# First cross attention of a decoder kernel: transposing a unit's attention weights as row halves of the array, with the copies on two engines

## The reference

```
scores  = einsum('bqhd,bkhd->bhqk', Q, K) / SCALE
weights = jax.nn.softmax(scores, axis=-1)
attn    = einsum('bhqk,bkhd->bqhd', weights, V).reshape(b, lq, h * d)
out     = attn @ Wo.T + bo
```

## Time and profile before

| | |
|---|---|
| median of 3 runs | 2547.52 us (2543.78 to 2550.26) |
| the profiled execution | 2545.91 us, with a span of 2543.8 us |
| busy share of the span | PE 89%, PEld 74%, DVE 64%, ACT 45%, POOL 29% |
| the 64 units of `stage_b` | scores from 810.6 us, last transposes at 1102.9 us |

### The profile page before, as it was taken

One profiled execution on the slowest core, in us unless ns is written; L12 is line 12 of the kernel. 1 busy time (PEld: TensorE's weight loads), 2 busy tenths in 40 slices (PEclk: granted clock), 3 DMA queues, 4 the chain that ended last, 5 costly groups with the idle time before them and its releaser, 6 DMA issues. The chain is left out here.

```text
span 2543.8 us, 62618 instructions
## 1 busy us (share of the span) xinstructions
PE 2262.9 (89%) x26115; PEld 1870.4 (74%) x26115; DVE 1633.5 (64%) x3577; ACT 1135.2 (45%) x3176; POOL 736.0 (29%) x866
## 2 busy tenths in 40 slices
PE   5798989998898999955998589989997899999998
PEld 4677877777785888844887366666775788888887
DVE  6766666667644667656784455655665777777776
ACT  4444443443324555522554356656674233333332
POOL 2333333424323433331565433420111011110110
PEclk9899999999999999966999799999998899999999
DMA  5000000100103000020442300000000000000001
GB/s 159 4 17 30 32 31 11 35 27 25 51 3 111 10 18 18 14 80 26 119 119 34 105 2 2 2 2 2 2 2 14 19 26 26 26 20 26 26 7 34
DMA packets 87961, 83.36 MB, mean 33 GB/s; under 512 B 27264, under 2 KB 83456, under 8 KB 86272
## 3 DMA queue, kind: packets, MB, share of 16 engines
q1 hardware_dynamic: 81536, 70.98, 8.9%
q0 software_dynamic: 6144, 8.39, 1.9%
HBM read 68.71 MB, written 10.65 MB: 31 GB/s over the span
## 5 line engine op out<-in xcount | busy, mean ns | idle before, releaser
L2653 PE MATMUL bank<-f_XH,f_wp 128*128 128x512 f32 x1088 | 364.6, 396 | 5.9 <-DVE f_XL L2763 5.9
L797 DVE SCALAR_TENSOR_TENSOR a_acc<-a_praw,a_convw,a_acc 128x256 f32<-128x256 f32 x345 | 206.7, 600 | 97.6 <-ACT a_acc L957 89.4
L2653 PEld LDWEIGHTS bank<-f_XH,f_wp 128*128 128x128 f32 x1088 | 208.4, 192 | 48.6 <-issue 5.0
L2653 PEld LDWEIGHTS bank<-f_wp,f_Hp 128*128 128x128 f32 x1632 | 214.3, 191 | 27.5 <-DVE X L2790 16.0
L2653 PE MATMUL bank<-f_wp,f_Hp 128*128 128x256 f32 x1632 | 218.5, 283 | 16.2 <-DVE X L2790 15.4
L2653 PE MATMUL bank<-f_XL,f_wp 128*128 128x512 f32 x544 | 215.9, 397 | 0.0
L2837 POOL TENSOR_TENSOR f_wp<-wa,f_wp 128x768 fp32r<-128x768 f32 x34 | 62.9, 1849 | 521.6 <-ACT f_wp L2803 521.6
L2788 DVE SCALAR_TENSOR_TENSOR X<-bank,f_w,X 128x256 f32<-128x256 f32 x512 | 211.4, 475 | 0.0
L2826 ACT ACTIVATE f_Hp<-f_H 128x512 fp32r<-128x512 f32 x136 | 85.9, 632 | 223.8 <-DVE f_H L2775 223.8
L2824 ACT ACTIVATE f_G<-bank 128x512 f32<-128x512 f32 x136 | 81.3, 598 | 165.2 <-PE bank L2653 165.2
L2777 DVE TENSOR_TENSOR f_Hp<-f_H,f_Hp 128x512 fp32r<-128x512 f32 x136 | 94.1, 692 | 94.9 <-ACT f_Hp L2826 94.9
(11 more groups left out here) (389 smaller groups left out, 5530.2 us busy)
## 6 DMA issues: line engine op xcount, KB each, us to landing
wa<-in_c_w SPq DMA_DIRECT2D x64, 256.0 KB, 3.4
wa<-in_f_gu SPq DMA_DIRECT2D x34, 256.0 KB, 2.8
wb<-grown SPq DMA_DIRECT2D x4, 1536.0 KB, 6.9
a_KQg<-grown SPq DMA_DIRECT2D x4, 1536.0 KB, 6.4
wa<-in_f_d SPq DMA_DIRECT2D x34, 128.0 KB, 2.8
a_E<-decays SPq DMA_DIRECT2D x16, 256.0 KB, 4.0
X<-in_x SPq DMA_DIRECT2D x4, 512.0 KB, 5.2
wa<-in_a_wqkv SPq DMA_DIRECT2D x1, 2048.0 KB, 8.8
```

The costliest lines, as they stand in the source:

```text
L797: i = v.e.scalar_tensor_tensor(A_, praw[:, c, :, j:j + BT_], convw[:, c, j:j + 1], A_, ALU.mult, ALU.add)
L2653: i = t.e.matmul(out_, lhsT[x], rhs[y], start=n == 0 and k == 0, stop=n == 2 and k == nk - 1, skip_group_check=True)
```

## The change

The transposes of a unit become one step `("turn", u)` with two banks, which stand for the two halves of the 128 tokens and no longer for the two `par`. Each of the 8 blocks of 128x77 is transposed as two blocks of 64x77, the first 64 tokens in the upper half of the array's rows, the other 64 in the lower half, each against a 64x64 part of the identity. The step waits for both banks before its first transpose, and both banks are filled by its last two. `b_PT` becomes two buffers of the same total size. DVE copies the first half's bank and ACT, right after its exps of the unit behind, copies the second half's bank.

```
-            PT = [t_(f"PT{i}", [HALF, 2, 2, P]) for i in range(NPB)]
+            PT = [t_(f"PT{i}", [HALF, 2, 2, 2, P]) for i in range(NPB // 2)]
-                order += [("turn", u - 2, par) for par in range(2)] * (0 <= u - 2 < U) + [("scale", u - 1)] * (0 <= u - 1 < U)
+                order += [("turn", u - 2)] * (0 <= u - 2 < U) + [("scale", u - 1)] * (0 <= u - 1 < U)
+                elif what == "turn":
+                    for half in range(2):
+                        at[s + (half,)] = banks[4 + turns % 4]
+                        at[s + (half,)].turn(*k, half)
+                        turns += 1
+                    continue
-            square = lambda ap: ap[0:HALF, :].rearrange("p (a b c) -> p a b c", a=2, b=2)
+            halves = [slice(0, P // 2), slice(P // 2, P)]
+            by_head = lambda ap: ap[0:HALF, :].rearrange("p (r a b c) -> p r a b c", r=2, a=2, b=2)
 # tensor, turn
-                        free(t, *s)
-                        for j in range(2):
-                            for hf in range(2):
-                                i = t.e.transpose(square(b.ap)[:, j, hf, :], Pm[u % NPB][:, par, j, hf * HALF:(hf + 1) * HALF], ident)
-                        i.then_inc(b.filled, 1)
+                        for half in range(2):
+                            free(t, *s, half)
+                        for par in range(2):
+                            for j in range(2):
+                                for hf in range(2):
+                                    for half, rows_ in enumerate(halves):
+                                        b = at[s + (half,)]
+                                        i = t.e.transpose(by_head(b.ap)[:, par, j, hf, :],
+                                                          Pm[u % NPB][rows_, par, j, hf * HALF:(hf + 1) * HALF],
+                                                          ident[rows_, rows_], tile_position=(rows_.start, 0))
+                                        if (par, j, hf) == (1, 1, 1):
+                                            i.then_inc(b.filled, 1)
 # tensor, mix: reads PT[u % 2][:, par, j, hf, :]
 # vector, turn
-                        filled(v, *s)
-                        v.e.tensor_copy(PT[2 * (u % 2) + par][:], square(b.ap)).then_inc(b.emptied, 1)
+                        filled(v, *s, 0)
+                        v.e.tensor_copy(PT[u % 2][:, :, :, :, halves[0]], by_head(b.ap)).then_inc(b.emptied, 1)
 # scalar, exp of unit u waits for both halves of turn u - 4; and new:
+                    elif what == "turn":
+                        u, b = s[1], at[s + (1,)]
+                        if u > 1:
+                            filled(c, "mix", u - 2)
+                        filled(c, *s, 1)
+                        c.e.activation(PT[u % 2][:, :, :, :, halves[1]], by_head(b.ap), ACT.Copy).then_inc(b.emptied, 1)
```

More of the change, by code:

```diff
@@ L1329, in tensor @@
                     elif what == "turn":
-                        _, u, par = s
+                        u = s[1]
                         t.wait_ge(scaled.sem, scaled.at[u,])
-                        free(t, *s)
-                        for j in range(2):
-                            for hf in range(2):
-                                i = t.e.transpose(square(b.ap)[:, j, hf, :], Pm[u % NPB][:, par, j, hf * HALF:(hf + 1) * HALF], ident)
-                        i.then_inc(b.filled, 1)
+                        for half in range(2):
[10 more added lines that the diff above has]
+                                            i.then_inc(b.filled, 1)
                     elif what == "mix":
@@ L1348, in tensor @@
                                     i = t.e.matmul(b.ap[rows(par), j * P:(j + 1) * P], V[:, n // TB, hf, 4 * q + 2 * j + par, :],
-                                                   PT[2 * (u % 2) + par][:, j, hf, :], start=hf == 0, stop=hf == 1,
+                                                   PT[u % 2][:, par, j, hf, :], start=hf == 0, stop=hf == 1,
                                                    tile_position=(0, par * XD), skip_group_check=True)
@@ L1403, in vector @@
                     elif what == "turn":
-                        _, u, par = s
+                        u, b = s[1], at[s + (0,)]
                         if u > 1:
                             filled(v, "mix", u - 2)
-                        filled(v, *s)
-                        v.e.tensor_copy(PT[2 * (u % 2) + par][:], square(b.ap)).then_inc(b.emptied, 1)
+                        filled(v, *s, 0)
+                        v.e.tensor_copy(PT[u % 2][:, :, :, :, halves[0]], by_head(b.ap)).then_inc(b.emptied, 1)
                     elif what == "mix":
@@ L1454, in scalar @@
                         if u >= NPB:
-                            filled(c, "turn", u - NPB, 1)
+                            for half in range(2):
+                                filled(c, "turn", u - NPB, half)
                             c.wait_ge(inverted.sem, inverted.at[u - NPB,])
```

## The result

The changed kernel took 2522.73 us in the median of 4 runs (2520.89 to 2528.92), the kernel before 2548.76 us beside it. The ratio is 0.991, with a 95% interval of 0.989 to 0.992: 20 to 27 us faster. The forecast was 2518 us, 29 us less, with a range of 2511 to 2535 us.

The account below looks back on a forecast made before the run. PE was taken as the bound. 54 units at 0.446 us (24.1 us) and 5.0 us for the last ten turns gave 29.1 us off 2545.91; with 1.6 us for the median, the forecast was 2518 us, range 2511 to 2535.

Parts of the forecast that it names:

- The start of the transposes: On PE, transposes start 0.63 us behind the score instead of 0.73, since both now share a tile shape.
- the mix: On PE, the mix starts 1.27 us into the round instead of 1.75, 0.48 us less.
- Rival A: On PE, the gap between score and transposes stays, as transposes may count as another shape: 2527 us, 15%.
- The price of a pair: On PE, two half-row transposes run beside each other and a pair goes by in 0.069 us.
- the upper bound: A pair of transposes at 0.112 us: mix at 1.57 us, 0.18 us a unit, 2536 us in all.
- PE stays the bound: In plain rounds of 3.21 us, POOL's scale feeds the transposes in time, by 0.12 us.
- rival B: PE no longer the bound: a longer copy, reciprocal and scale loop costs 0.1 to 0.2 us a round, 2524 to 2531 us, 12%.
- The three rounds with a layernorm: Of every eight rounds, three with waits on POOL gain 0.33 + 0.48 + 0.36 = 1.17 of 12.54 us.
- The last ten units: Ten turns at the stage's end, where queries are missing, together gain 5.0 us.
- rival C: PE's clock falls to half earlier, in the three rounds of 3.48 us, as PE waits more: 2526 us, 7%.
- Rival D: On PE, the two transposes of a pair do not overlap: 14 us slower, 2561 us, 6%.
- E: No change: PE held by the number of instructions, 0.062 us a transpose, 0.03 us gained a unit: 2545 us, 2%.

Follow-up runs that it names:

- experiment 5: Changed kernel with PE doing the mix before the transposes in units 8 to 51: 2524.47 us in one run.
- experiment 9: Changed kernel with 64 instead of 77 stationary columns in each transpose, part of the attention left out: 2509.93 us in one run.
- experiment 4: Changed kernel with 8 of a unit's 16 transposes taking 128 stationary columns instead of 77: 2517.74 us in one run.
- experiment 8: Changed kernel with DVE's reciprocal ahead of the copy and the next stage's layernorm moved a round later: 2511.05 us, ratio 0.986 to the kernel before.
- experiment 1: Changed kernel with half-row transposes but both copies on DVE, none on ACT: 2543.94 us, ratio 0.999 to the kernel before.
- experiments 6: Changed kernel with DVE's reciprocal of the unit behind moved ahead of the copy of the transposes: 2520.12 us, ratio 0.988 to the kernel before.
- 7: Changed kernel with the first score matmuls of units 57 to 63 repeated to fill PE's waits: 2521.93 us, ratio 0.989 to the kernel before.
- experiment 3: Changed kernel with all 8 transposes of one row half first, then the other 8, instead of alternating: 2541.82 us in one run.
- experiment 2: Kernel before, whole-array transposes kept, only the second bank's copy moved to ACT: 2539.76 us, ratio 0.998 to the kernel before.

## Why the prediction was right, and where not

**The start of the transposes** at 0.63 us and **the mix** at 1.27 were worked out, 0.63 and 1.26 to 1.27 measured; the round 3.20 against 3.21. Rival A is out, and experiment 5 shows the rule at work: one more change of shape in a round costs the 0.15 us.

**The price of a pair**, 0.069 us, was right. That it hangs on the number of stationary columns is shown by experiment 9 for 64 against 77 (0.056 us, near the lower bound of 0.0575). The rule behind it, a pair goes by the wider of load and pass with the load priced by its columns, does not hold to the end: the upper bound, 0.112, was taken from matmuls, and experiment 4 shows that a half-row transpose with 128 columns goes by in about 0.067 us.

**PE stays the bound** by 0.12 us was worked out, with 0.05 us from POOL's end to the transposes taken off. In plain rounds the scale ends 0.15 to 0.17 us before the transposes start, so the margin is 0.10 to 0.12, and rival B is out. The prediction did not price what the second engine is worth: with both copies on DVE the margin is negative, and of 21.6 us in units 8 to 55 only 9.1 are left. The copy on ACT is not a detail of the change but more than half of it.

**The three rounds with a layernorm**, 1.17 us gained, one wait kept and one gone: 12.54 - 11.37 = 1.17 us measured. Experiment 8 shows that POOL's order sets the kept wait.

**The last ten units**, 5.0 us, is the term that was mis-sized: 1.0 us measured. The loop of these rounds shrank nearly as worked out (3.48 to 2.98 us, forecast 2.91). The sum took half clock for two turns and a saving of 1.3 us in them, as before the change. What it missed is a second stretch of half clock behind the last score, 1081.5 to 1091.7 us, in which the way from the last transposes to the layernorm grew from 12.40 to 16.02 us. This is rival C's cause, the clock, and its sign was met (1.00 left before 1065 us; it was 1064.4), but at less than half its price of 8 us and not by its account: in the three rounds the clock held. The first fall came in unit 61's round, as in the kernel before, and cost nothing net (0.46 us gained from the score of 61 to that of 63). Where the fall does come in the three rounds is experiment 1 (1065.3 us, behind the score of unit 57), the kernel in which PE waits for POOL in most rounds. That less idle time of PE takes these stretches away is shown by one profile each of experiments 6 (the second) and 7 (both); what decides when the clock falls is not shown.

**Rival D** (no overlap) and **E** (a cost for each instruction) are out: 16 transposes took 0.71 us from the first start to the last end, and even unordered ones overlap.

The sum: 29.1 us forecast, 24.6 us in the stage, 20 to 27 us by the timed ratio. Nearly all of the difference is that one term.

## What to carry to other kernels

When a step on the full engine gets shorter, work out the loop of the other engines that feeds it first: here, over 48 units, 0.48 us off PE's group was worth 9 us alone, a copy moved to an idle engine 2 us alone, and both together 22. Put groups of one tile shape behind each other, and alternate the halves of the rows. And where the full engine will now wait, look at the granted clock there and behind it: shorter work can lose part of its gain to the clock, and a variant whose clock happens to hold can look better than it is. So compare stretches at the same clock.

## What was not expected of the hardware

- Transposes on half the rows step by 0.056 us with 64 stationary columns and by 0.069 with 77, but by about 0.067 with 128 (experiment 9, the change itself, experiment 4); half-row float32 matmuls step by 0.112 with 128.
- Transposes on the free half of the rows start ahead of earlier ones on the busy half: in experiment 3 ahead of the last three of eight.
- With one wait of the same length (1.53 and 1.52 us) in the same round, the clock fell in the kernel before and held in experiment 2.
- The first stage, the same in all these kernels, ends at times that differ by up to 10 us: the first score started at 809.1 to 819.0 us in the twelve profiles of the experiments. In the windows view the granted clock of the first 800 us is 0.93 or 0.94 in the early ones and 0.92 in those that end at 818 us or later. Much of the spread between runs may come from there; no run was made to show it.
